# First attention of a two-layer block: four result buffers, maxima tiles issued one at a time, and the diagonal mask added by VectorE

## The reference, cut to what matters

```python
A1 = einsum('bhqd,bhkd->bhqk', Q1, K1) * scaling     # 16 numbers per head and half
A2 = einsum('bhqd,bhkd->bhqk', Q2, K2) * scaling
A1 = where(causal, A1, -inf); A2 = where(causal, A2, -inf)
attn = softmax(A1, -1) - lam * softmax(A2, -1)
O = einsum('bhqk,bhkd->bhqd', attn, V)
```

## Time and profile before

| | |
|---|---|
| median of 3 runs | 4490.27 us (4481.56 to 4502.51) |
| the profiled execution | 4483.99 us, span of its records 4481.8 us |
| mean granted TensorE clock | 0.902 |
| PE busy | 3649.0 us, 81% of the span |
| DVE busy | 2374.4 us, 53% |
| ACT busy | 1656.8 us, 37% |
| POOL busy | 1702.6 us, 38% |
| first maxima of head 0 begin | 306.7 us |
| line 803 of head 0 and of head 31 | 349.6 and 2695.6 us |

### The profile page before, as it was taken

How to read it: one execution, slowest core, us unless ns; L and a number is a source line. 1 busy time by engine, 2 the same in 40 slices (tenths; PEclk the granted TensorE clock), 3 DMA queues, 4 the chain that set the end, 5 groups by cost and what they waited for, 6 DMA issues and landing times. The chain is left out here.

```text
span 4481.8 us, 84217 instructions
## 1 busy us (share of the span) xinstructions
PE 3649.0 (81%) x28333; PEld 1946.0 (43%) x28335; DVE 2374.4 (53%) x4499; ACT 1656.8 (37%) x3266; POOL 1702.6 (38%) x1117
## 2 busy tenths in 40 slices
PE   6868888998988888888898897762799768897694
PEld 3323344443434343434344443662455434555463
DVE  4457566565656565656566560776511176666202
ACT  2314555555555555555555555110022132111110
POOL 1313454554545454545454555420144332110112
PEclk8978999999999999999999998775699989997797
DMA  4430101111111111111111111210233310001333
GB/s 151 154 113 24 41 25 42 26 40 28 38 30 35 32 34 34 31 37 25 42 26 40 27 26 51 103 48 11 90 90 76 59 34 4 0 0 38 108 100 92
DMA packets 229259, 224.74 MB, mean 50 GB/s; under 512 B 88721, under 2 KB 198546, under 8 KB 222738
## 3 DMA queue, kind: packets, MB, share of 16 engines
q1 hardware_dynamic: 213522, 194.33, 14.7%
q0 software_dynamic: 15360, 25.44, 2.9%
HBM read 138.58 MB, written 80.35 MB: 49 GB/s over the span
## 5 line engine op out<-in xcount | busy, mean ns | idle before, releaser
L692 DVE TENSOR_REDUCE attention_chunk_max<-attention_ps_m 128x1 f32<-128x512 f32 (+3 forms) x2560 | 1386.9, 603 | 892.1 <-PE attention_ps_m L795 451.0
L637 POOL TENSOR_TENSOR attention_probs<-attention_probs 128x1024 f32<-128x1024 f32 (+2 forms) x640 | 1225.9, 1916 | 1281.5 <-PE attention_ps_o L770 1281.5
L670 ACT ACTIVATE attention_probs<-attention_ps_s 128x512 f32<-128x512 f32 (+3 forms) x2560 | 1241.6, 536 | 939.3 <-PE attention_ps_s L745 481.9
L741 PE MATMUL attention_ps_s<-attention_q_stack,attention_k_stack 99*128 99x512 bf16 (+3 forms) x2560 | 836.6, 358 | 176.3 <-ACT attention_probs L670 155.5
L792 PE MATMUL attention_ps_m<-attention_k_stack,attention_q_stack 96*128 96x512 bf16 (+3 forms) x2560 | 811.3, 360 | 152.6 <-DVE attention_chunk_max L692 98.4
L770 PE MATMUL attention_ps_o<-attention_probs,attention_v_head 128*32 128x256 f32 (+1 forms) x9728 | 657.4, 376 | 0.5 <-ACT attention_probs L670 0.4
L792 PEld LDWEIGHTS attention_ps_m<-attention_k_stack,attention_q_stack 96*128 96x128 bf16 x2560 | 248.5, 99 | 524.5 <-DVE attention_chunk_max L692 357.7
L741 PEld LDWEIGHTS attention_ps_s<-attention_q_stack,attention_k_stack 99*128 99x128 bf16 x2560 | 223.2, 98 | 524.1 <-ACT attention_probs L670 259.3
L781 PE MATMUL attention_ps_o<-attention_probs,consts 128*32 128x256 f32 (+1 forms) x5120 | 432.6, 369 | 0.4 <-POOL attention_probs L637 0.4
L770 PEld LDWEIGHTS attention_ps_o<-attention_probs,attention_v_head 128*32 128x32 f32 x9728 | 268.1, 112 | 273.7 <-ACT attention_probs L670 100.4
L781 PEld LDWEIGHTS attention_ps_o<-attention_probs,consts 128*32 128x32 f32 x5120 | 204.4, 113 | 90.3 <-issue 13.5
(11 more groups left out here) (276 smaller groups left out, 3979.6 us busy)
## 6 DMA issues: line engine op xcount, KB each, us to landing
qk_parts<-project_parts SPq DMA_DIRECT2D x64, 384.0 KB, 3.0
heads_out<-attention_results_sb SPq DMA_DIRECT2D x256, 64.0 KB
out_heads<-heads_out SPq DMA_DIRECT2D x8, 2048.0 KB, 7.9
experts_w<-in_f_w SPq DMA_DIRECT2D x16, 1024.0 KB, 8.3
attention_q_stack<-qk_parts SPq DMA_DIRECT2D x32, 384.0 KB
attention_k_stack<-qk_parts SPq DMA_DIRECT2D x32, 384.0 KB
experts_w<-in_e_w SPq DMA_DIRECT2D x24, 512.0 KB, 4.9
v_rows<-project_v SPq DMA_DIRECT2D x8, 1024.0 KB
```

Source lines behind the costliest of these rows:

```text
L637: pool.tensor_tensor(probs[:, to, :, lo:], probs[:, to, :, lo:], probs[:, k % RING_P, :, lo:], ALU.add).then_inc(pair_ok, 1)
L670: act.activation(probs[:, k % RING_P, a, left(k):], ps_s[(2 * k + a) % RING_S][:, left(k):], ACT.Exp, scale=float(DH) ** -0.5).then_inc(pr ...
L692: last = dve.tensor_reduce(chunk_max[:, a, jq, c:c + 1], ps_m[m % RING_M][:, 0:width(m)], AX.X, ALU.max)
L741: last = pe.matmul(psum[:, lo:], ks[at][0:WITH_MAX, a, kb * P:(kb + 1) * P], qs[at][0:WITH_MAX, a, tq * GROUP + lo:(tq + 1) * GROUP], star ...
```

## The change

In the stage `attention0`: `results_sb` gets four slots, one for each query tile (PSUM keeps two), and the copy by ACT moves one score later (from before the second half of step 3, 7, 15 or 27 to before the first half of the next step). The mask matmuls of the maxima (line 795) go; in their place DVE runs, for the 32 diagonal tiles, one `tensor_tensor_reduce` that adds a mask from SBUF and takes the maximum, and that also writes the masked tile back to PSUM. The maxima of a pair of steps are dealt out in four shares instead of three, with one share behind the two first scores, one behind the third, one behind the strips and one behind the fourth score. The three-part split of the maxima keeps its rest in PSUM. `mask_q_bf` is no longer made.

```diff
@@ -501,16 +499,16 @@
 
 
     with stage(nc, "attention0") as s:
-        RING_P, RING_S, RING_M, RING_O = 8, 3, 3, 2
+        RING_P, RING_S, RING_M, RING_O, RING_R = 8, 3, 3, 2, 4
         qs = [s.sb(f"q_stack{i}", [P, 2, N], BF16) for i in range(STACKS)]
         ks = [s.sb(f"k_stack{i}", [P, 2, N], BF16) for i in range(STACKS)]
         vh = [s.sb(f"v_head{i}", [P, K_TILES, DV], F32) for i in range(STACKS)]
         probs = s.sb("probs", [P, RING_P, 2, GROUP], F32)
-        results = s.sb("results_sb", [P, RING_O, 2, BLOCKS, P], F32)
+        results = s.sb("results_sb", [P, RING_R, 2, BLOCKS, P], F32)
+        mask_wide = s.sb("mask_wide", [P, GROUP], F32)
...
         max_parts = s.sb("max_parts", [2 * K_TILES, 3, P], BF16)
-        max_rest = s.sb("max_rest", [2 * K_TILES, P], F32)
         ps_s = [s.ps(f"ps_s{i}", [P, GROUP]) for i in range(RING_S)]
         ps_m = [s.ps(f"ps_m{i}", [P, GROUP]) for i in range(RING_M)]
         ps_o = [s.ps(f"ps_o{i}", [P, 2, BLOCKS, P]) for i in range(RING_O)]
...
@@ -606,7 +604,7 @@
 
             def store(head, turn):
 
-                tile, slot = TURNS[turn - 1], (turn - 1) % RING_O
+                tile, slot = TURNS[turn - 1], (turn - 1) % RING_R
                 h = head - 1 if turn == 0 else head
                 h = h if isinstance(h, int) else sp.snap(h)
                 wait_apart(sp, taken, head * Q_TILES + turn + RING_O, core.passed)
...
@@ -645,14 +643,11 @@
             act.sem_inc(taken, RING_O)
 
             def take(head, turn):
-                slot = turn % RING_O
-                if isinstance(head, int):
-                    act.wait_ge(stored[slot], ((head * Q_TILES + turn) // RING_O + 1) * (STORES * 16))
-                else:
-                    act.wait_ge(stored[slot], (head * (Q_TILES // RING_O) + turn // RING_O + 1) * (STORES * 16))
+                slot = turn % RING_R
+                act.wait_ge(stored[slot], (head * (Q_TILES // RING_R) + 1) * (STORES * 16))
                 act.wait_ge(values_ok, head * N_STEPS + LAST[turn] + 1)
                 act.wait_ge(ones_ok, head * PAIRS + (LAST[turn] + 1) // PAIR + RING_P // PAIR)
-                act.activation(results[:, slot], ps_o[slot][:], ACT.Copy).then_inc(taken, 1)
+                act.activation(results[:, slot], ps_o[turn % RING_O][:], ACT.Copy).then_inc(taken, 1)
 
             def step(at_head, after, later):
                 if at_head is None:
...
@@ -660,8 +655,8 @@
                 head = at_head.n
                 for k in range(N_STEPS):
                     for a in range(2):
-                        ended = ends(k, 4)
-                        if a == 1 and ended and not (ended[1] and is_first(head)):
+                        ended = ends(k, 5)
+                        if a == 0 and ended and not (ended[1] and is_first(head)):
                             take(head - 1 if ended[1] else head, ended[0])
                         act.wait_ge(score_ok, head * 2 * N_STEPS + 2 * k + a + 1)
                         if k % PAIR == 0 and a == 0:
...
@@ -680,6 +675,8 @@
 
                 dve.memset(ks[i][STACK:P], 1.0)
                 dve.memset(qs[i][STACK:P], 0.0)
+            dve.memset(mask_wide[:, 0:GROUP - P], 0.0)
+            dve.tensor_copy(mask_wide[:, GROUP - P:], core.c("mask_q"))
 
             dve.memset(chunk_max[:], -3.0e38).then_inc(ready, 1)
             dve.sem_inc(max_used, RING_M)
...
@@ -688,26 +685,31 @@
             def maxima(after, items):
                 for m in items:
                     a, jq, c = MAXIMA[m]
-                    dve.wait_ge(max_ok, after * N_MAX + m + 1)
-                    last = dve.tensor_reduce(chunk_max[:, a, jq, c:c + 1], ps_m[m % RING_M][:, 0:width(m)], AX.X,
-                                             ALU.max)
+                    w, to = width(m), chunk_max[:, a, jq, c:c + 1]
+                    if c == jq // GT:
+                        wait_apart(dve, max_ok, after * N_MAX + m + 1, core.passed)
+                        last = dve.tensor_tensor_reduce(ps_m[m % RING_M][:, 0:w], ps_m[m % RING_M][:, 0:w],
+                                                        mask_wide[:, GROUP - w:], 1.0, -3.0e38, ALU.add, ALU.max, to)
+                    else:
+                        dve.wait_ge(max_ok, after * N_MAX + m + 1)
+                        last = dve.tensor_reduce(to, ps_m[m % RING_M][:, 0:w], AX.X, ALU.max)
                     last.then_inc(max_used, 1)
                     if m == len(MAXIMA) - 1:
                         dve.wait_ge(max_used, after * N_MAX + m + 1 + RING_M)
                         dve.tensor_reduce(neg_max[:], chunk_max[:].rearrange("p a j c -> p (a j) c"), AX.X, ALU.max,
                                           negate=True).then_inc(neg_ok, 1)
 
-                        chain = Counted(dve, steps, after * 2)
+                        chain = Counted(dve, steps, after * 4)
                         m = len(MAXIMA)
                         psum = ps_m[m % RING_M][0:2 * K_TILES, 0:P]
                         dve.wait_ge(max_ok, after * N_MAX + m + 1)
                         dve.wait_ge(parts_in, (after + 1) * 48)
                         chain.then(dve.tensor_copy(max_parts[:, 0], psum))
-                        dve.tensor_tensor(max_rest[:], psum, max_parts[:, 0], ALU.subtract).then_inc(max_used, 1)
-                        dve.wait_ge(max_used, after * N_MAX + m + 1 + RING_M)
-                        chain.then(dve.tensor_copy(max_parts[:, 1], max_rest[:]))
-                        dve.tensor_tensor(max_parts[:, 2], max_rest[:], max_parts[:, 1], ALU.subtract)\
-                            .then_inc(parts_ok, 1)
+                        chain.then(dve.tensor_tensor(psum, psum, max_parts[:, 0], ALU.subtract))
+                        chain.then(dve.tensor_copy(max_parts[:, 1], psum))
+                        chain.then(dve.tensor_tensor(max_parts[:, 2], psum, max_parts[:, 1], ALU.subtract))
+                        dve.sem_inc(parts_ok, 1)
+                        dve.sem_inc(max_used, 1)
 
             def step(at_head, next_head, later):
                 if at_head is None:
...
@@ -788,13 +790,8 @@
                     a, jq, c = MAXIMA[m]
                     w = width(m)
                     pe.wait_ge(max_used, after * N_MAX + m + 1)
-                    diagonal = c == jq // GT
-                    last = pe.matmul(ps_m[m % RING_M][:, 0:w], qs[at][0:STACK, a, jq * P:(jq + 1) * P],
-                                     ks[at][0:STACK, a, c * GROUP:c * GROUP + w], start=True, stop=not diagonal)
-                    if diagonal:
-                        last = pe.matmul(ps_m[m % RING_M][:, w - P:w], core.ident_bf[:], core.mask_q_bf[:],
-                                         start=False, stop=True)
-                    last.then_inc(max_ok, 1)
+                    pe.matmul(ps_m[m % RING_M][:, 0:w], qs[at][0:STACK, a, jq * P:(jq + 1) * P],
+                              ks[at][0:STACK, a, c * GROUP:c * GROUP + w], start=True, stop=True).then_inc(max_ok, 1)
 
             def turn_maxima(after):
                 m = len(MAXIMA)
...
@@ -824,30 +821,31 @@
                     if whose is not None and (k == BEGIN_MAX or k == 0 and is_first(head)):
                         pe.wait_ge(loaded[whose_at], (whose.round + 1) * (LOADS * 16))
                     more = k + 2 < N_STEPS
-                    third = -(-len(items) // 3)
+                    share = [items[n * len(items) // 4:(n + 1) * len(items) // 4] for n in range(4)]
                     if more:
                         score(head, at, k + 2, 0)
-                        maxima(whose_n, whose_at, items[:third])
                         score(head, at, k + 2, 1)
-                        maxima(whose_n, whose_at, items[third:2 * third])
+                    maxima(whose_n, whose_at, share[0])
+                    if more:
                         score(head, at, k + 3, 0)
                     elif after is not None:
 
                         pe.wait_ge(parts_in, (after + 2) * 48)
-                        maxima(whose_n, whose_at, items[:2 * third])
                         score(after, other, 0, 0)
+                        score(after, other, 0, 1)
+                    maxima(whose_n, whose_at, share[1])
                     values(head, at, k)
                     values(head, at, k + 1)
                     if k > 0:
                         ones(head, k // PAIR - 1)
                     elif not is_first(head):
                         ones(head - 1, PAIRS - 1)
+                    maxima(whose_n, whose_at, share[2])
                     if more:
                         score(head, at, k + 3, 1)
                     elif after is not None:
-                        score(after, other, 0, 1)
                         score(after, other, 1, 0)
-                    maxima(whose_n, whose_at, items[2 * third:])
+                    maxima(whose_n, whose_at, share[3])
                     if after is not None and k == END_MAX:
```

(10 more changed lines are left out.)

## The result

The changed kernel takes 4081.56 us (median of 4 runs, 4076.47 to 4082.61) against 4491.16 us (4 runs): a ratio of 0.9085, 95% interval 0.9062 to 0.9107. The forecast was 4139 us, the range 4080 to 4230, so the time lies 1.6 us above its lower end: the store wait went as forecast, two terms were mis-sized by a lot and a cost appeared that the sum did not have. The profiled execution took 4081.09 us.

What follows compares the result with a forecast made beforehand. PE was taken to bound an undisturbed head, with 8.0 us lost in each other head through ACT's wait for a store. 4484 - 232 - 57 - 63 + 7 = 4139 us, range 4080 to 4230.

Steps and rivals of the forecast that it cites:

- the store wait: In the attention stage ACT waits for a store issued behind a head's loads, 6.1 us each, and PE waits behind ACT.
- Four slots: Result copies by ACT no longer wait for a late store; 29 periods become as head 30's, 29 x 8.0 = 232 us.
- rival 4: The slots free nothing because the stores as such are too slow for the stage: 4371 us, chance 3%.
- Nothing late next: Loads that PE asks for at step 20 are in time, by 3 us, so nothing is counted: 0.
- rival 2: Loads end some 2 us past the mark (line 803) in every head and PE idles: 100 us, 4240 us, chance 6%.
- Maxima one at a time: PE waits less for DVE to free maxima tiles: 2.1 of 3.1 us a head, 30 x 2.1 = 63 us.
- Mask matmuls: Mask matmuls dropped from PE: 32 x 0.06 = 1.9 us a head, 30 x 1.9 = 57 us.
- VectorE's masked maximum: DVE adds the diagonal masks, hidden beside PE; only the 80 maxima before head 0 cost, + 7 us (0 to 18).
- rival 1: DVE's masked maximum runs at half rate: +18 us a head on DVE, local waits of about 2 us, 4210 us, chance 11%.
- rival 3: VectorE becomes the bound, its mask read from SBUF held up and its rate halved: 85.8 us a head, 4830 us, chance 3%.
- periods of 64 to 65 us: Sign expected in the trace: the once-a-head mark (line 803) comes every 64 to 65 us; over 68 would be wrong.

## Why the prediction was right, and where its sizes were off

**Four slots**, forecast 232 us: right. With them alone heads that hold no loop end have 68.5 us, 8.0 less than the mean before. The term itself came to (76.5 - 69.65) x 29 = 199 us with the loop ends in it, and the medians differ by 202, which also rules out rival 4.

**Nothing late next**, forecast 0: wrong by about 45 us. The loads were in time, as counted (no wait for them in front of step 20), so rival 2 did not come. The step that failed is the 0 itself: only the loads were looked at. The store wait had covered the 8 loop ends: its end was tied to the store's landing, so 2 us of idle time in front of it cost nothing. Uncovered, 3.4 us idle and the slow clock behind them make a period 66.2 to 67.6 us instead of 61.2, 8 x 5.6 = 45 us. No loop gave 43 us back and six heads a pass 27 (22.5 by the marks).

**Maxima one at a time**, forecast 63 us: the term that was off most. It came to 5.9 us a head where VectorE leaves the mask to PE (68.5 to 62.6) and 7.5 with the changed kernel's mask, against 2.1. The step that failed is "in head 30 PE waits 3.1 us for DVE to free a maxima tile, 10 times". The row is right, and it isn't the loss. A matmul of 512 columns is drawn 0.38 us long, but its follower can start 0.22 behind it, so the first 0.16 us of a wait behind it show as work. Two neighbours of the kernel before:

```profile
1561.75 0.38 PE L792 MATMUL attention_ps_m<-attention_k_stack,attention_q_stack 96*128 96x512 bf16 x1
1562.36 0.28 PE L792 MATMUL attention_ps_m<-attention_k_stack,attention_q_stack 96*128 96x256 bf16 x1 [0.23 <-DVE attention_chunk_max L692]
```

They start 0.61 apart where 0.22 would do: 0.39 are lost and 0.23 shown. The weight loads, which are short, show more of it in the same head 30:

```profile
PEld attention_ps_m L792 <- DVE attention_chunk_max L692: 10.4, 20, 1.4
```

20 waits and not 10; the true loss, 5.9, lies between this row (which also counts time that a matmul covers) and the earlier trace rows. The distances of starts give it: in head 30, 39 maxima tiles follow directly on another or on its mask, 17 of them start late, and against the shortest distance for their widths 6.2 us are lost, of which 3.1 are drawn as idle time, at 10 of the 17. With the new order 5 such neighbours are left and lose nothing; in the changed kernel with the old order it is 7.0 us, where the run gives 7.5.

**Mask matmuls**, forecast 57 us: right in sign only together with the order, and too large. It is 1.2 us a head with the new order, and 21 us between the medians; with the old order it is a loss (18 us slower alone). Two steps failed. The 0.06 us behind a mask was taken as all that it adds, and what the maxima tile in front of it then needs was left out. And I had called PE the bound of head 30, where in the old order the ring held PE back.

**VectorE's masked maximum**, forecast + 7 us in the open: the 80 maxima of head 0 take 42.6 us against 42.1, and DVE's busy time in head 30 is 46.4 us, not 52.9. The second instruction overlaps its neighbours, so the + 0.17 us for it was not there. The 512-column tile takes 702 ns where half the rate would make some 1200, so rival 1, and with it rival 3, is out.

The parts fit the trace. From the marks, heads 1 to 29 are 2218.3 - 1819.5 = 398.8 us shorter, head 30 is 7.3 shorter, and the rest 3.5 longer: 402.6 of the 402.9 us between the two profiled executions. By cause: -232 for the wait, 30 x (68.5 - 61.2) = -219 for order and mask in 30 heads (5.9 and 1.4, by the quiet head of the order alone; the masks are 1.2 of the 1.4, and the rest isn't assigned to the split or the copy), + 45 for the loop ends, + 3.5. Forecast were -232, -120, 0 and +7. Too small a gain of the order and a missing loop end made up for each other in part, which kept the time in the range. That was luck: had the loop ends cost nothing, as forecast, the time would have been the 4038 us of the kernel without a loop, and outside. The wait and what ends it were right; the sizes of the two terms on PE were not, nor were the periods of 64 to 65 us (61.2 measured).

## What to carry to other kernels

Before a wait is taken away, ask what else stands in front of its end: idle time that a later, fixed landing hides costs nothing until the wait goes, and is full price then. Read what a small wait costs from the distance of two starts, not from the idle column, where the engine's instructions are drawn longer than their spacing; 7 of the 17 late starts in head 30 show no idle time at all. And before work is taken from the busiest engine, see whether a ring paces it: here the same 32 matmuls were worth -0.4, or +1.2 us a head, depending on where the tiles stood between the strips.

## What the runs showed of the hardware

A jump back to the start of the loop left PE idle for 1.9 to 3.8 us each time that the traces show it, and in the changed kernel the granted clock was 0.50 for some 6 us afterwards; 32 heads written out, without a jump, ran with PE busy for 99.8% of 1774 us. An output read from VectorE's accumulator adds a record of 142 ns behind its instruction and 8 ns between starts (606 against 598 for 512 columns). A cast of 32 x 128 took some 910 to 1020 ns from SBUF in the 31 heads where a GpSimd addition was running, and ended 74 to 81 ns after that addition each time; it took 214 ns in the one head with GpSimd idle, and 278 to 280 from PSUM in either case.
